# A layer of Mamba, MoE and attention on one core: the Mamba front written out over five turns, its scan's diagonals made by DMA, and the router's normalised rows on ScalarE

## The chip, the cores and the metric

The kernel runs on one core of a Trainium2 chip. A core has TensorE (PE, matrix products and transposes), VectorE (DVE), ScalarE (ACT), GpSimd (POOL) and SyncE (SP), which issues DMA transfers. Each engine works through its own instructions in order, and they wait for each other by semaphores. The metric is the device time of one launch in microseconds (us). Lower is better.

## The reference, cut to what matters

The input x is 8 sequences of 512 tokens with 128 features. Four blocks follow each other, each with its layer norm and residual: Mamba, a mixture of experts, attention, and the same mixture of experts again. The change touches the Mamba block and the first router behind it:

```
x   = x + mamba(layernorm(x))
    xn    = x * rsqrt(mean(x*x) + eps) * norm_w            # x is layernorm(x) here
    x_s,z = split(xn @ in_proj_w.T)                        # 256 channels each
    u     = silu(causal_conv4(x_s) + conv_b)
    dt,B,C = split(u @ x_proj_w.T)                         # 8, 16, 16 columns
    delta = softplus(dt @ dt_proj_w.T + dt_proj_b)
    for each of 16 states s:  h_t = exp(delta*A_s)*h_{t-1} + delta*u*B_s ;  y += h*C_s
    y     = (y + u*D) * silu(z)
    out   = y @ out_proj_w.T + x
x   = x + moe(layernorm(x))     # router: argmax and softmax of layernorm(x) @ gate_w, 8 experts
x   = x + attention(layernorm(x)) ; x = x + moe(layernorm(x))
```

The residual of the Mamba block adds x and layernorm(x), so x is replaced by x(1+rstd) - mean*rstd before the block's output is added.

## The kernel before

Tokens lie on 128 partitions, in 32 tiles (`NT`) of 128 tokens, four of them (`TPB`) to a batch of 512 tokens. Channels number 256, as two chunks (`NC`) of 128 partitions.

**setup** loads x in four parts, takes each tile's mean and variance on DVE (`bn_stats`, then `bn_aggr`, then two copies for each batch), builds the table of the attention bias (`ext`) on DVE, and from the variances the factors `rr` (both reciprocal roots) and `r12`. A barrier ends it.

**mamba_front** computes `u`, the gates `zs`, `delta`, `du` = delta*u and the B columns `bT` of each batch, and leaves all in a large SBUF tile called `arena`. PE, DVE, ACT, POOL and SP each have a loop of hardware (`Fori`) over the batches with peeled first and last turns. In a turn b DVE runs `normed(b+2)` (L424, four tiles), `conved(b+1)` (L451, six operations), `lows(b)` (L479), `deltas` (L463, the positive part of delta), a copy of B (L473), `residual(b+2)` (L438, four tiles of x(1+rstd) - mean*rstd) and `bounds(b)` (L484, the minimum that ends the log1p). POOL does four 128x1024 operations for a batch: L608 and L611 make the log1p's sum from what `lows` left, L614 adds the positive part to give delta, L618 multiplies by u. L614 needs `bounds` of the same batch. `delta_ln`, `delta_low` and `delta_pos` have one buffer each.

**mamba_scan** runs over n = 16b + s: 128 steps, one state s of one batch b each. A step is: ACT scales du by B into `b_du` (L730, four tiles, two buffers) and makes exp(delta*A) in `d_a` (L738, two operations, two buffers); PE transposes the four tiles into PSUM, `p_dbu` (L834, two buffers); DVE scans 128x1024 into `h` (L954, six buffers); POOL multiplies by the C row (L690), which SP has loaded with a DMA for each step (four buffers); PE adds the product up (L854), four steps behind the first. For s in `DIAG` = (1, 3, 11, 15) ACT instead scales four 128x128 identity tiles (a diagonal of B), and PE multiplies du with that diagonal (L831).

Between the steps stands other work on earlier batches, placed by s. For batch b-1: DVE gates the sum at s=2 (L961), copies at s=5, 6, 8 and 9, adds the residual at s=7 (L967), takes the router's moments at s=8; ACT makes the router's `rstd` at s=10; POOL makes the router's normalised rows at s=10 (`pool_rows`, L1246, four tiles); PE turns these rows at s=13 (L1206), ACT copies them at s=14 (L1186), PE forms the logits at s=14 (L1212), ACT copies x at s=15 (L1200). For batch b-2: the rest of the router, ending in four indirect DMAs from POOL at s=7 (`pool_send`, L1259).

The waits that the prediction speaks of are these. `exps` of step n waits for the end of scan n-2 (`scanned, n - 1`), and so does PE's `spread`; scan n waits for `exps` and `spread` of n and for the product n-6 to be added up; each engine takes its own list strictly in order.

## Time and profile before

| | |
|---|---|
| median of 3 runs | 1271.05 us (1267.11 to 1273.8) |
| the profiled execution: its time | 1267.82 us |
| its span, first to last instruction | 1266.0 us |
| around the span | 1.82 us |
| mean granted TensorE clock | 0.948 |
| busy over the span: PE / DVE / ACT / POOL | 84% / 73% / 68% / 42% |
| setup | 0 to about 20 us |
| front | 24.6 us (first work on DVE) to 151.9 us |
| scan | 158.9 us (first scan) to 531.4 us |
| from there: end of the router, experts, attention, experts | to 1266.0 us |

The scan of step 0 of batches 0 to 6 starts at 158.87, 202.60, 247.73, 296.07, 343.01, 390.17 and 437.30 us. Busy shares are averages over stages with unlike limits, so a stage has to be read by itself.

### The profile page before, as it was taken

The page shows a single profiled execution, that of the slowest core. Times are in us where ns is not written, and L with a number is a line of the kernel's source. Part 1 is how long each engine was busy: PE and PEld are TensorE (multiplying, and loading weights), DVE is VectorE, ACT ScalarE, POOL GpSimd, SP SyncE. Part 2 cuts the span into 40 slices and gives each one's busy share as a digit, 9 for nine tenths or more (in the row PEclk, how much of TensorE's full clock was granted, in tenths as well). Part 3 has the DMA queues.
Part 4 walks back from the last instruction along what each step waited for, and adds up shares of the span by engine and source line. Part 5 has one row for each costly group of instructions (what it writes and reads, how often), then busy time and mean ns, then how long its engine had stood idle before and what let it go on. Part 6 is the DMA issues. An engine that isn't in the chain of part 4 may idle for free. (4 is left out here: it accounts for less than half of the span.)

```text
span 1266.0 us, 25040 instructions
## 1 busy us (share of the span) xinstructions
PE 1064.5 (84%) x7486; PEld 758.3 (60%) x7486; DVE 925.9 (73%) x2001; ACT 866.4 (68%) x1837; POOL 533.2 (42%) x361
## 2 busy tenths in 40 slices
PE   1776399988888888769967999998999999993897
PEld 0333278888887888639963455544454545542897
DVE  5899588998898898845644777767685868674565
ACT  1777599999999999635642757565675657661564
POOL 0366478989999999733440001010101010111344
PEclk9988799999999999988997999998999999997899
DMA  3000023233364354223322000000000000001331
GB/s 89 2 2 3 35 77 97 92 96 101 116 204 136 110 187 124 67 75 97 91 72 58 1 2 18 1 19 1 17 0 19 1 17 1 17 18 55 90 89 52
DMA packets 50631, 74.40 MB, mean 59 GB/s; under 512 B 7351, under 2 KB 28604, under 8 KB 50528
## 3 DMA queue, kind: packets, MB, share of 16 engines
q1 hardware_dynamic: 41648, 51.22, 13.9%
q0 software_dynamic: 5568, 12.66, 2.8%
q10 hardware_dynamic: 3312, 9.33, 2.3%
q8 instruction: 41, 0.67, 0.2%
q14 instruction: 62, 0.51, 0.1%
HBM read 57.86 MB, written 16.24 MB: 59 GB/s over the span
## 5 line engine op out<-in xcount | busy, mean ns | idle before, releaser
L954 DVE TENSOR_TENSOR_SCAN h<-d_a,p_dbu 128x1024 f32<-128x1024 f32 x128 | 290.2, 2280 | 37.3 <-ACT d_a L738 33.0
L690 POOL TENSOR_TENSOR h<-h,c_rep 128x1024 f32<-128x1024 f32 x126 | 295.1, 2366 | 25.1 <-DVE h L954 23.7
L1894 ACT ACTIVATE arena<-arena,at_min 128x512 f32<-128x512 f32 x256 | 183.2, 720 | 118.5 <-DVE at_min L2005 114.9
L2005 DVE CUSTOM_DVE_ANT_0 arena<-at_p_scores,arena 128x512 f32<-128x512 f32 x256 | 174.6, 685 | 83.2 <-PE at_p_scores L1769 41.8
L1255 POOL TENSOR_SCALAR r_row<-r_row 128x4 f32<-128x4 f32 x16 | 3.8, 239 | 472.9 <-DVEq L1160 472.9
L1776 PEld LDWEIGHTS at_p_probs_T<-ident,arena 128*128 128x128 f32 x1024 | 113.1, 142 | 97.2 <-issue 73.9
L738 ACT ACTIVATE d_a<-arena,a_exp 128x511 f32<-128x511 f32 x256 | 169.2, 709 | 0.2 <-DVE h L954 0.2
L1769 PE MATMUL at_p_scores<-arena,at_q_T 64*128 64x512 f32 x512 | 161.8, 646 | 6.9 <-DVE at_min L2005 5.3
L1776 PE MATMUL at_p_probs_T<-ident,arena 128*128 128x128 f32 x1024 | 159.0, 284 | 5.2 <-ACT arena L1894 4.8
L730 ACT ACTIVATE b_du_T<-arena,b_T 128x256 f32<-128x256 f32 x384 | 162.6, 495 | 0.1
L854 PE MATMUL p_y_T<-ident,h 128*128 128x128 f32 x1024 | 133.6, 274 | 5.0 <-POOL h L690 4.9
L854 PEld LDWEIGHTS p_y_T<-ident,h 128*128 128x128 f32 x1024 | 115.9, 141 | 7.2 <-POOL h L690 6.6
L834 PE MATMUL p_dbu<-ident,b_du_T 128*128 128x128 f32 x768 | 114.4, 284 | 5.0 <-ACT b_du_T L730 3.5
L2014 DVE COPY at_probs_T<-at_p_probs_T 128x512 f32<-128x512 f32 x128 | 88.1, 688 | 31.2 <-PE at_p_probs_T L1776 31.1
L1861 ACT ACTIVATE at_probs_T<-at_p_probs_T 128x512 f32<-128x512 f32 x128 | 75.6, 591 | 38.4 <-PE at_p_probs_T L1776 36.1
L834 PEld LDWEIGHTS p_dbu<-ident,b_du_T 128*128 128x128 f32 x768 | 86.5, 143 | 22.3 <-ACT b_du_T L730 9.7
L1436 PE MATMUL f_p_h<-f_xg_T,f_w_cur 128*128 128x128 f32 x624 | 88.2, 287 | 5.9 <-DVE f_w_cur L1492 5.5
L1472 ACT ACTIVATE f_h_T<-f_p_h,f_w_cur 128x128 f32<-128x128 f32 x312 | 88.8, 374 | 4.3 <-PE f_p_h L1436 3.4
L1448 PE MATMUL f_p_y<-f_w_cur,f_h_T 128*128 128x128 f32 x624 | 84.2, 279 | 0.7 <-issue 0.7
L1436 PEld LDWEIGHTS f_p_h<-f_xg_T,f_w_cur 128*128 128x128 f32 x624 | 78.9, 199 | 8.5 <-issue 6.8
L1769 PEld LDWEIGHTS at_p_scores<-arena,at_q_T 64*128 64x128 f32 x512 | 43.8, 187 | 61.8 <-issue 45.0
L1448 PEld LDWEIGHTS f_p_y<-f_w_cur,f_h_T 128*128 128x128 f32 x624 | 77.2, 195 | 1.3 <-issue 1.1
(242 smaller groups left out, 1661.3 us busy)
## 6 DMA issues: line engine op xcount, KB each, us to landing
c_rep<-c_rows SPq DMA_DIRECT2D x128, 256.0 KB, 3.2
f_row<-expert_rows SPq DMA_DIRECT2D x78, 129.0 KB
arena<-in_w_all ACTq DMA_DIRECT2D x8, 578.0 KB
arena<-bias_by_distance ACTq DMA_DIRECT2D x8, 448.0 KB
x_tok<-in_x SPq DMA_DIRECT2D x4, 512.0 KB, 5.6
x_tok<-x_between SPq DMA_DIRECT2D x8, 256.0 KB, 2.7
expert_rows<-r_row,r_dest POOLq DMA_INDIRECT x64
expert_rows<-h SPq DMA_DIRECT2D x6, 129.0 KB
```

Source lines behind the costliest of these rows:

```text
L690: nc.gpsimd.tensor_tensor(h[:, n % HS, :, :], h[:, n % HS, :, :], cc, ALU.mult).then_inc(prod_done, 1)
L730: nc.scalar.activation(b_du[:, s % SR, j, 0:width], src, ACT.Copy, scale=bT[:, one(b), j, s:s + 1].squeeze(1)).then_inc(scaled, 1)
L738: nc.scalar.activation(da[:, s % 2, ch, 1:], delta[:, one(b), ch, 1:].squeeze(1), ACT.Exp, scale=a_exp[:, ch, s:s + 1]).then_inc(da_ready, 1)
L834: mm = nc.tensor.transpose(dst, b_du[:, s % SR, j, ch * P:(ch + 1) * P], k.ident[:])
L854: mm = nc.tensor.matmul(p_yT[:, j, ch * P:(ch + 1) * P], h[:, n % HS, ch, j * P:(j + 1) * P], k.ident[:], is_transpose=SUM_BY_TRANSPOSE, s ...
L954: nc.vector.tensor_tensor_scan(h[:, n % HS, :, :].rearrange("p c t -> p (c t)"), da[:, s % 2, :, :].rearrange("p c t -> p (c t)"), p_dbu[: ...
L1436: mm = nc.tensor.matmul(ph[:, r % R, f, :], w_cur[:, r % R, f * P:(f + 1) * P], xgT[:, r % R, :], start=True, stop=True)
L1448: mm = nc.tensor.matmul(py[:, r % YR, 0:D], ht[:, r % R, f, :], w_cur[:, r % R, FF + f * D:FF + (f + 1) * D], start=f == 0, stop=f == FC - 1)
L1769: nc.tensor.matmul(psc[:, n % SCB, :], qT[par][half, hd // 2, it * P:(it + 1) * P], kT[par][half, hd // 2, :], start=True, stop=True).then ...
L1776: mm = nc.tensor.transpose(ppt[:, s % 2, j * P:(j + 1) * P], pr[:, s % RING, j * P:(j + 1) * P], k.ident[:])
L1894: nc.scalar.activation(pr[:, slot, :], sc[:, slot, :], ACT.Exp, scale=-1.0, bias=mn[:, slot:slot + 1]).then_inc(probs_ready, 1)
L2005: V.tensor_tensor_reduce(sc[:, slot, :], psc[:, s % SCB, :], band[:, hd, w0:w0 + T], 1.0, 3.0e38, ALU.add, ALU.min, mn[:, slot:slot + 1]). ...
```

## The change

1. **setup.** `bn_aggr` writes straight into a tile that is kept, its two copies go, and it runs one batch behind `bn_stats`. The bias table is made by ACT (three operations and a negation) and its zeroing by POOL. The factors 1+rstd, -mean*rstd and `rn` are made at the end of setup. The weights of the Mamba block are loaded here, not in the front.
2. **mamba_front.** All loops are written out. Every engine runs through turns i = -3 to 7, in which each piece works on its own batch i + offset. The residual is made before the normalised x: for batches 0 to 3 by DVE in `normed`, for 4 to 7 by ACT, with 16 operations that are the first of the front. `delta_pos` has two buffers, the log1p its own buffer `lm`, and POOL makes delta and du one turn later than the sums.
3. **mamba_scan, diagonals.** For the 30 steps from n=8 on with s in `DIAG` (`BY_DIAG`) ACT makes no diagonal. SP writes four B values of each partition to the diagonals of a 128x128x4 block in DRAM that is zero otherwise (four such blocks, zeroed once at the start), seven steps ahead, and loads the block into `diag_b` four steps ahead (two buffers). Both stand in the queue of the C rows.
4. **mamba_scan, router's rows.** `pool_rows` goes. DVE makes -mean*rstd (128x4) behind scan 10, `stage == 3`, and ACT makes the rows with scale and bias (`act_normed`) behind the exponentials of s=11.

```diff
@@ setup
-                    for j in range(TPB):
-                        ch.step(V.bn_stats(stats[:, b % 2, j, :], k.x[:, g + j, :]))
-                    ch.wait()
-                    for j in range(TPB):
-                        ch.step(V.bn_aggr(mv[:, b % 2, j, :], stats[:, b % 2, j, :]))
-                    ch.wait()
-                    ch.step(V.tensor_copy(k.mean[:, g:g + TPB], mv[:, b % 2, :, 0]))
-                    ch.step(V.tensor_copy(var[:, g:g + TPB], mv[:, b % 2, :, 1]))
+            for b in range(B):
+                if b % (B // PARTS) == 0:
+                    dve.wait_ge(x_in[b // (B // PARTS)], 16)
+                parts_of(b)
+                if b > 0:
+                    moments_of(b - 1, TPB)
@@ mamba_front, the turns
+        def each(*parts):
+            for i in range(-3, B):
+                for ahead, part in parts:
+                    if 0 <= i + ahead < B:
+                        part(i + ahead)
...
+            each((0, dt_proj), (2, project_in), (1, x_proj), (3, turn))                                    # PE
+            each((1, conved), (0, positive), (-1, bounds), (0, take_b), (3, normed), (0, lows))            # DVE
+            each((1, first_tap), (0, xd_out), (2, x_out), (1, gates), (0, absolute), (1, u_out), (0, logs))  # ACT
+            each((0, log_sums), (-1, delta_du))                                                            # POOL
@@ mamba_front, DVE
+            def positive(b):
+                after(dve, delta_done, b - 1)
+                for ch in range(NC):
+                    dve.wait_ge(abs_ready, b * NC + ch + 1)
+                    nc.vector.tensor_scalar(mpos[:, b % 2, ch, :], pdt[:, ch, :], dt_b(ch), 0.0,
+                                            ALU.add, ALU.max).then_inc(pos_ready, 1)
+            def bounds(b):
+                if b == B - 1:
+                    return
+                dve.wait_ge(log_sum_ready, b + 1)
+                after(dve, delta_done, b)
+                nc.vector.tensor_tensor(lm[:], low[:], ex[:], ALU.min).then_inc(log1p_ready, 1)
@@ mamba_front, ACT
+            for g in range(NT // 2, NT):
+                nc.scalar.activation(k.x[:, g, :], k.x[:, g, :], ACT.Identity, scale=k.one_plus[:, g:g + 1],
+                                     bias=k.shift[:, g:g + 1]).then_inc(half_added, 1)
@@ mamba_scan, SP
+            def write_diagonal(i):
+                b, s = divmod(BY_DIAG[i], NS)
+                if i >= DR:
+                    sp.wait_ge(diag_in[(i - DR) % DB], 16 * ((i - DR) // DB + 1))
+                dst = bass.AP(diag_rows.tensor, i % DR * TPB * P * P, [[P + 1, P], [P * P, TPB], [1, 1]])
+                sp.dma_start(dst, bT[:, b, :, s:s + 1], allow_slow_non_contiguous=True).then_inc(diag_out[i % DR], 16)
+            def read_diagonal(i):
+                sp.wait_ge(diag_out[i % DR], 16 * (i // DR + 1))
+                if i >= DB:
+                    sp.wait_ge(dbu_ready, BY_DIAG[i - DB] + 1)
+                sp.dma_start(diag_b[:, i % DB, :, :],
+                             diag_rows[i % DR].rearrange("j k m -> k j m")).then_inc(diag_in[i % DB], 16)
@@ mamba_scan, POOL and ACT
-                    if s == 10 and b > 0:
-                        rt.pool_rows(pool, b - 1)
+                if n in BY_DIAG:
+                    return
...
+                    if number > 0 and s == 11:
+                        rt.act_normed(act, b - 1)
@@ Router
+        elif stage == 3 and self.in_psum:
+            dve.wait_ge(self.rstd_ready, 1 + b)
+            V.scalar_tensor_tensor(out=self.shift, in0=self.mv[:, :, 0], scalar=-1.0, in1=self.rstd,
+                                   op0=ALU.mult, op1=ALU.mult).then_inc(self.shift_ready, 1)
+    def act_normed(self, act, b):
+        act.wait_ge(self.shift_ready, 1 + b)
+        self.rows_out(act, b)
+        for j in range(TPB):
+            ins = self.k.nc.scalar.activation(self.row[:, j, 0:D], self.k.x[:, b * TPB + j, :], ACT.Identity,
+                                              scale=self.rstd[:, j:j + 1], bias=self.shift[:, j:j + 1])
+        ins.then_inc(self.ln_ready, 1)
```

How the order of instructions moves is shown at three places. The first is POOL in the front: before, this is the loop's body (sum of the log1p in L608 and L611, delta in L614, du in L618, all of one batch).

```order
L608 TENSOR_TENSOR delta_low<-delta_e,delta_low 128x1024
L609 REGISTER_ALU
L611 TENSOR_TENSOR delta_low<-delta_low,delta_ln 128x1024
L614 ISA
L614 TENSOR_TENSOR arena<-delta_ln,delta_pos 128x1024
L616 ISA
L618 ISA
L618 TENSOR_TENSOR arena<-arena 128x1024
```

After, POOL's first ten operations of the front are these (L572 and L575 the sums, L563 delta, L566 du).

```order
L572 TENSOR_TENSOR delta_low<-delta_e,delta_low 128x1024
L575 TENSOR_TENSOR delta_low<-delta_low,delta_ln 128x1024
L572 TENSOR_TENSOR delta_low<-delta_e,delta_low 128x1024
L575 TENSOR_TENSOR delta_low<-delta_low,delta_ln 128x1024
L563 TENSOR_TENSOR arena<-delta_log1p,delta_pos 128x1024
L566 TENSOR_TENSOR arena<-arena 128x1024
L572 TENSOR_TENSOR delta_low<-delta_e,delta_low 128x1024
L575 TENSOR_TENSOR delta_low<-delta_low,delta_ln 128x1024
L563 TENSOR_TENSOR arena<-delta_log1p,delta_pos 128x1024
L566 TENSOR_TENSOR arena<-arena 128x1024
```

The sums of a batch now stand directly ahead of delta and du of the batch before it, and DVE's minimum of the earlier batch falls under them. DVE's own turn of the front is this after the change, here a turn that still normalises (L455 `conved`, L468 `positive`, L487 `bounds`, L473 the B columns, L441 `normed`, L479 `lows`).

```order
L455 SCALAR_TENSOR_TENSOR conv<-p_xz,vec,conv 128x511 x2
L455 SCALAR_TENSOR_TENSOR conv<-p_xz,vec,conv 128x510 x2
L455 SCALAR_TENSOR_TENSOR conv<-p_xz,vec,conv 128x509 x2
L468 TENSOR_SCALAR delta_pos<-p_dt,vec 128x512 x2
L487 TENSOR_TENSOR delta_log1p<-delta_low,delta_e 128x1024
L473 COPY b_T<-p_xdbc 128x64
L441 TENSOR_SCALAR xn_tok<-x_tok,mean_and_var,rn 128x128 x4
L479 TENSOR_SCALAR delta_low<-delta_e 128x1024
```

The residual has left the turn, `lows` has gone from its middle to its end, and the minimum stands after `positive`. The second place is ACT in the scan from s=10 to s=15 of a batch: before, with the diagonals from `ident` at s=11 and s=15.

```order
L1182 ACTIVATE r_rstd<-r_lnv 128x4
L738 ACTIVATE d_a<-arena,a_exp 128x511 x2
L730 ACTIVATE b_du_T<-ident,b_T 128x128 x4
L738 ACTIVATE d_a<-arena,a_exp 128x511 x2
L730 ACTIVATE b_du_T<-arena,b_T 128x256 x4
L738 ACTIVATE d_a<-arena,a_exp 128x511 x2
L730 ACTIVATE b_du_T<-arena,b_T 128x256 x4
L738 ACTIVATE d_a<-arena,a_exp 128x511 x2
L730 ACTIVATE b_du_T<-arena,b_T 128x256 x4
L1186 ACTIVATE arena<-p_r_x 128x512
```

After, over the same steps (L722 the scaling, L730 the exponentials, L1192 the router's rows, L1198 the copy at s=14).

```order
L1186 ACTIVATE r_rstd<-r_lnv 128x4
L730 ACTIVATE d_a<-arena,a_exp 128x511 x4
L1192 ACTIVATE r_row<-x_tok,r_veps,r_rstd 128x128 x4
L722 ACTIVATE b_du_T<-arena,b_T 128x256 x4
L730 ACTIVATE d_a<-arena,a_exp 128x511 x2
L722 ACTIVATE b_du_T<-arena,b_T 128x256 x4
L730 ACTIVATE d_a<-arena,a_exp 128x511 x2
L722 ACTIVATE b_du_T<-arena,b_T 128x256 x4
L1198 ACTIVATE arena<-p_r_x 128x512
```

The four diagonal tiles are gone, and four row tiles stand ahead of the scaling of s=12. The third place is DVE behind scan 10, after the change (L953 is the scan; before, the same list has no L1115 and the scans stand in one row).

```order
L974 COPY arena<-p_r_x 128x2x256
L953 SCALAR_TENSOR_TENSOR h<-d_a,p_dbu 128x1024
L974 COPY arena<-p_r_x 128x2x256
L953 SCALAR_TENSOR_TENSOR h<-d_a,p_dbu 128x1024
L1115 SCALAR_TENSOR_TENSOR r_veps<-r_mv,r_rstd 128x4
L953 SCALAR_TENSOR_TENSOR h<-d_a,p_dbu 128x1024 x4
```

One small operation with both inputs in SBUF now stands between scan 10 and scan 11.

## Rows read from the trace of the kernel before

**Rows 1.** Windows: busy us by engine, one batch of the scan (s=10 to s=10).
```profile
373.29:420.45 47.16, 41.45 (x356) 38.41 (x355) 42.24 (x45) 45.29 (x102) 44.71 (x26) 1.00 0.44 139
```

**Rows 2.** Timeline, DVE, setup and first turn: start, us, engine, line, operation, count [idle before].
```profile
5.08 0.87 DVE L246 BATCH_NORM_STATS2 n_stats<-x_tok 128x6 f32<-128x128 f32 x4 [1.73 <-DMA x_tok<-in_x]
...
19.38 0.19 DVE L268 TENSOR_TENSOR r<-rstd_and_rms 128x32 f32<-128x32 f32 x1 [0.61 <-ACT rstd_and_rms L223]
...
24.84 1.11 DVE L424 TENSOR_SCALAR xn_tok<-x_tok,mean,r 128x128 f32<-128x128 f32 x4
...
47.76 0.69 DVE L479 TENSOR_SCALAR delta_low<-delta_e 128x1024 f32<-128x1024 f32 x1 [0.62 <-ACT delta_e L577]
```

**Rows 3.** Timeline, PE, first projections of the front.
```profile
28.01 3.78 PE L368 MATMUL p_xz<-xn_T,w_in 128*128 128x512 f32 x4 [0.83 <-ACT xn_T L536]
...
31.59 3.20 PE L362 MATMUL p_xz<-w_in,xn_T 128*128 128x256 f32 x8
```

**Rows 4.** Timeline, DVE, one turn of the front's loop.
```profile
76.32 0.68 DVE L479 TENSOR_SCALAR delta_low<-delta_e 128x1024 f32<-128x1024 f32 x1
76.92 1.40 DVE L463 TENSOR_SCALAR delta_pos<-p_dt,vec 128x512 f32<-128x512 f32 x2
...
78.37 4.09 DVE L438 TENSOR_SCALAR x_tok<-x_tok,one_plus_rstd,mean_rstd  x4
82.37 1.22 DVE L484 TENSOR_TENSOR delta_ln<-delta_low,delta_e 128x1024 f32<-128x1024 f32 x1
...
86.58 4.02 DVE L451 SCALAR_TENSOR_TENSOR conv<-p_xz,vec,conv 128x511 f32<-128x511 f32 x6
```

**Rows 5.** Timeline, POOL, the same turn.
```profile
77.08 2.36 POOL L608 TENSOR_TENSOR delta_low<-delta_e,delta_low 128x1024 f32<-128x1024 f32 x1 [2.39 <-DVE delta_low L479]
...
86.70 2.37 POOL L618 TENSOR_TENSOR arena<-arena  x1 [0.38 <-POOL arena L614]
```

**Rows 6.** One line: ns min/median/max of one, first and last start (us).
```profile
L1012 DVE TENSOR_TENSOR h<-h,c_rep x2: 1212/1468/1723, 531.5 to 533.2; 128x1024 f32<-128x1024 f32 x2
```

**Rows 7.** Timeline, POOL, the end of the scan.
```profile
522.90 9.29 POOL L690 TENSOR_TENSOR h<-h,c_rep 128x1024 f32<-128x1024 f32 x4
```

**Rows 8.** Timeline, DVE, the last operation of the front.
```profile
150.68 1.23 DVE L520 TENSOR_TENSOR arena<-arena 128x1024 f32<-128x1024 f32 x1
```

**Rows 9.** Timeline, DVE, scans 10 to 13, 14, 15 and 0.
```profile
373.29 8.88 DVE L954 TENSOR_TENSOR_SCAN h<-d_a,p_dbu 128x1024 f32<-128x1024 f32 x4
384.20 2.29 DVE L954 TENSOR_TENSOR_SCAN h<-d_a,p_dbu 128x1024 f32<-128x1024 f32 x1 [2.03 <-ACT d_a L738]
...
387.79 2.29 DVE L954 TENSOR_TENSOR_SCAN h<-d_a,p_dbu 128x1024 f32<-128x1024 f32 x1 [1.22 <-ACT d_a L738]
...
390.17 2.28 DVE L954 TENSOR_TENSOR_SCAN h<-d_a,p_dbu 128x1024 f32<-128x1024 f32 x1
```

**Rows 10.** Timeline, ACT, s=14 to s=1 of the same batch.
```profile
382.35 0.60 ACT L1186 ACTIVATE arena<-p_r_x 128x512 f32<-128x512 f32 x1 [0.91 <-PE p_r_x L1206]
...
385.76 1.32 ACT L738 ACTIVATE d_a<-arena,a_exp 128x511 f32<-128x511 f32 x2
386.98 1.69 ACT L730 ACTIVATE b_du_T<-arena,b_T 128x256 f32<-128x256 f32 x4
388.58 1.33 ACT L738 ACTIVATE d_a<-arena,a_exp 128x511 f32<-128x511 f32 x2
389.81 1.27 ACT L730 ACTIVATE b_du_T<-ident,b_T 128x128 f32<-128x128 f32 x4
```

**Rows 11.** Timeline, POOL, s=10 on, and behind the next batch's indirect DMAs.
```profile
378.40 3.14 POOL L1246 TENSOR_SCALAR r_row<-x_tok,r_mv,r_rstd 128x128 f32<-128x128 f32 x4
381.52 27.98 POOL L690 TENSOR_TENSOR h<-h,c_rep 128x1024 f32<-128x1024 f32 x12
...
418.52 4.71 POOL L690 TENSOR_TENSOR h<-h,c_rep 128x1024 f32<-128x1024 f32 x2
```

**Rows 12.** DMA issues: KB each, median us from issue to landing.
```profile
c_rep<-c_rows SPq DMA_DIRECT2D x128, 256.0 KB, 3.2
```

More of the change, by code:

```diff
@@ L263, in _, with parts_of, moments_of @@
-            ch.link(V.tensor_scalar(args[:, 0, :], var[:], LN_EPS, None, ALU.add))
+            def parts_of(b):
+                for j in range(TPB):
+                    ch.step(V.bn_stats(stats[:, b, j, :], k.x[:, b * TPB + j, :]))
+            def moments_of(b, back):
+                ch.wait(back)
+                for j in range(TPB):
+                    ch.step(V.bn_aggr(k.mv[:, b * TPB + j, :], stats[:, b, j, :]))
+            for b in range(B):
[4 more added lines that the diff above has]
+                    moments_of(b - 1, TPB)
@@ L332, in _ @@
[L332 to L340 removed]
+            for b in range(B):
+                sp.wait_ge(xd_ready, b + 1)
+                sp.dma_start(cscr[b], xd[C_AT:C_AT + NS, :]).then_inc(c_stored, 16)
@@ new lines, in project_z, with project_in @@
+            def project_z(b):
+                pe.wait_ge(xnT_ready, b + 1)
+                after(pe, z_taken, b * NC)
+                for j in range(TPB):
+                    at = j % 2 * DI
+                    mm = nc.tensor.matmul(pz[:, NC + j // 2, at:at + DI], xnT[:, j * P:(j + 1) * P], w_in[:, DI:],
+                                          start=True, stop=True)
+                    if j % 2:
+                        mm.then_inc(z_half_ready, 1)
+            def project_in(b):
+                if b == 0:
+                    project_x(b)
+                    project_z(b)
+                else:
+                    project_z(b)
+                    project_x(b)
@@ L419, in normed @@
             def normed(b):
-                dve.wait_ge(xT_ready, b)
+                if b < B // 2:
+                    for g in range(b * TPB, b * TPB + TPB):
+                        chn.step(nc.vector.tensor_scalar(k.x[:, g, :], k.x[:, g, :], k.one_plus[:, g:g + 1],
+                                                         k.shift[:, g:g + 1], ALU.mult, ALU.add))
+                    chn.wait()
+                else:
+                    dve.wait_ge(half_added, (b - B // 2 + 1) * TPB)
+                after(dve, xT_ready, b)
@@ L431, in residual @@
-            def residual(b):
-                dve.wait_ge(xn_ready, b + 1)
-                chn.wait()
-                for j in range(TPB):
-                    g = b * TPB + j
-                    xg = k.x[:, one(g), :].squeeze(1)
-                    chn.step(nc.vector.tensor_scalar(xg, xg, rone[:, one(g)], mr[:, one(g)],
-                                                     ALU.mult, ALU.subtract))
+                ins.then_inc(xn_ready, 1)
             def conved(b):
@@ L487, in _ @@
-            residual(0)
-            conved(0)
-            normed(1)
-            residual(1)
-            def turn(b, conv_next=True, norm_next=True):
-                if norm_next:
-                    normed(b + 2)
-                if conv_next:
-                    conved(b + 1)
-                lows(b)
-                deltas_and_b(b)
-                if norm_next:
-                    residual(b + 2)
-                bounds(b)
-            with dve.Fori(0, B - 2) as b:
-                chn.begin(b, 11)
-                turn(b)
@@ L629, in mamba_scan @@
     DIAG = (1, 3, 11, 15)
+    BY_DIAG = [n for n in range(NS // 2, B * NS) if n % NS in DIAG]
+    DR, DB = 4, 2
     HALF = T // 2
```

346 lines of the change are left out of this document (146 added, 200 removed).

## Prediction

> **What bounds the kernel now.** I read the page's slices first: no engine is busy throughout, so the stages were read apart, by windows and then by timelines of one turn and one batch. About 0.5% (6.4 us) is what a measurement of this kernel can tell from no change.
>
> In the front DVE sets the pace. A turn takes 14.21 us (`lows` at 76.32 [rows 4], the next `lows` at 90.53, which is 86.58 + 3.95 [rows 4]). The reader is to see that much of it is not DVE's own work: four x_tok operations take 4.09 us [rows 4], where four like them take 1.11 us with POOL idle [rows 2]. POOL is at its 128x1024 operations then [rows 5], so a DVE operation from SBUF to SBUF waits for the end of POOL's operation. Operations that read PSUM show nothing of it: the six of conv take 4.02 us, 0.67 each, with POOL at L618 from 86.70 on [rows 4, 5].
>
> In the scan a batch takes 47.16 us (373.29 to 420.45), with ACT busy 45.29, POOL 44.71, DVE 42.24, PE 41.45 of it [rows 1]. Scans 10 to 13 follow each other at 2.22 us; then DVE stalls 2.03 and 1.22 us ahead of scans 14 and 15 [rows 9]. The chain behind that: POOL makes the router's rows at 378.40 to 381.52 [rows 11], PE turns them, ACT waits 0.91 us for it [rows 10], and the exponentials of s=14 stand behind that copy.
>
> **The change, part by part.**
>
> *Setup.* Now a batch of statistics takes 0.87 us for four [rows 2] within a period of 1.46; without copies and waits I take 1.13. With the bias table gone from DVE (0.9) and 0.8 added at the end for the new factors, DVE ends at about 17.2 instead of 19.57 [rows 2]. A barrier costs 1.1 us (150.68 + 1.23 = 151.91 [rows 8], next block 153.0). The weights are there, so the front begins at 18.3, not at 24.8 [rows 2]: 6.5 us earlier.
>
> *Start of the front.* The 6.5 us don't arrive. ACT's 16 residual tiles come first: a 128x128 tile costs 0.29 (four in 1.27 with their overlap [rows 10]), so 4.7 us, until 23.0. The first projection starts at about 23.7 instead of 28.01 [rows 3], 4.3 earlier. But x_proj(0) now stands behind the whole projection of batch 1, whose two halves take 3.78 and 3.20 us at the low clock of the start [rows 3], about 5 us as the clock rises, and `gates(0)` ahead of `u_out(0)`. Following the lists I put x_dbc(0) at 40.1 and `lows(0)`'s end at 48.1. Before it ended at 48.45 [rows 2]. Gain 0.3.
>
> *A turn.* Turn 1 is ACT's: its list adds up to 10.8 us with two table loads; `lows(1)` ends at 59.0. From turn 2 on POOL and DVE form a loop. Count from the end of `lows(i-1)`: two sums, delta(i-2) and du(i-2), each 2.36 and 0.08 apart, 0.38 ahead of du [rows 5]: delta done at 7.3, du running from 7.7 to 10.1. `positive(i)` waits for delta(i-2) (two buffers) and takes until 8.7 (1.40 for two, less 0.07 of overlap [rows 4]). Next is `bounds`, with both inputs in SBUF. Does POOL hold it up? Its 1.22 in the loop [rows 4] doesn't tell, since POOL then waits for it. L1012 does: of two equal products one takes 1212 ns and the other, begun at 531.5, 1723 ns [rows 6], and POOL's last product ended at 522.90 + 9.29 = 532.19 [rows 7]. 532.19 plus 1.2 is 533.4, near its end at 533.25. So `bounds` runs from 10.1 to 11.3; the copy of B, four unblocked `normed` (1.11 [rows 2]) and `lows` (0.68 [rows 4]) end at 13.25. ACT's exponential waits for `bounds` and is done at 12.5, in time. Turns 2 to 4 take 13.25, turns 5 and 6 (no `normed`, but that exponential) 13.15. In turn 7 delta(6) holds `lows(7)` until 13.7, du(6) holds the first operation of the tail until 16.7, and five operations of 1.23 [rows 8] end 22.85 after `lows(6)`. Sum: 59.0 + 39.75 + 26.3 + 22.85 = 147.9 against 151.9 [rows 8]. The front gives 4.0 us. Were `bounds` not held, a turn would take 11.9 and the tail less: 138, a gain of 14.
>
> The Trainium skill states the lock in so many words (SBUF — State Buffer, "SBUF: two separate sides"): VectorE with two SBUF inputs, or in a two-port mode, and GpSimd each take a shared pair of ports for a whole instruction, and the other waits. It speaks against this change; by it the front gives the smaller figure. The trace agrees, 1723 against 1212 ns.
>
> *Diagonals.* ACT loses 4 x 0.29 = 1.17 us in 30 steps. In batch 0, where ACT alone sets the pace (2.82 a step: 1.22 from 385.76 to 386.98 and 1.60 on to 388.58 [rows 10]), both steps count: 43.7 becomes 41.4, -2.3. SP's new transfers are each issued steps ahead. Their cost is not in the trace; the nearest row is a C row's 3.2 us for 256 KB [rows 12], the same size as a diagonal's load. Zeroing hides under the wait for the first product. At s=15 the C row stands behind a load that waits for `spread(15)`, which makes POOL's product some 1.8 us late where PE needs it 3 steps later: nothing. Low bound 0; high bound, were a write of 512 single elements to take three times 3.2 us, about 1 us a batch from SP's blocked C rows, 7 us. I take 0.
>
> *Router's rows.* POOL loses 3.1 us [rows 11] and the stall of 2.03 + 1.22 goes. In its place comes a wait: the small operation stands behind scan 10, and ACT, which would have scaled s=12 under scan 10, waits for it. Count from scan 10's end. The small operation has two SBUF inputs, and POOL is catching up behind its indirect DMAs, back to back from 418.52 at 2.33 a product [rows 11] (27.98 for twelve [rows 11]); its second ends at 423.2, scan 10 (420.45, the end of [rows 1]) at 422.7: held 0.5. Rows 0.7 to 1.9; scaling 12 to 3.5; exponentials 12 ready at 4.8, where scan 12 could have begun at 2.8: stall 2.0. ACT then needs 2.82 a step for 13 and 14 against 2.22 of the scan, and the copy of s=14 between: scans 13, 14, 15 and 0 begin at 7.7, 11.0, 13.3 and 15.7. Before, scan 0 began 14.7 after scan 10's end (390.17 - 375.5 [rows 9]). So +1.0. From s=0 to s=10 DVE's own list and its wait for the gate, which hangs on PE and on `scanned`, take what they took; two stalls of 0.2 and 0.24 for late diagonals may go: -0.3 to -0.4. A batch: +0.6 or +0.7. Batch 1, ACT-bound at 45.1 (starts listed with the profile), comes to 45.7: +0.6. Batch 2, 48.3 before, to 47.8: -0.5. Batches 3 to 7: +3.5. With batch 0's -2.3 the scan comes to +1.3.
>
> *Behind the scan* nothing is changed; POOL's products end earlier, but DVE's chain after scan 15 is its own.
>
> Sum: -4.0 + 1.3 = -2.7. Against the profiled execution's 1267.8 that is 1265.1; the median of the runs lies 3.2 above that execution, so 1268.
>
> **The rivals.**
>
> 1. *`bounds` isn't held* (0.2). Against it: [rows 6, 7], though one operation is thin. -14 in the front instead of -4: 1258.
> 2. *The scan falls to POOL's pace* (0.1). POOL's load after the change is 16 x 2.33 + 6.0 for the send = 43.3 a batch, ACT's 41.8, DVE's 42.3. If the wait for scan 10 hid, six batches would give 3.7 each, -22: 1245. For it: all four engines would be below 43.5. Against: the count above, each step of it in program order.
> 3. *Slower: the small operation is held for a whole product* (0.15). If POOL has just begun a product at scan 10's end, DVE and ACT wait 2.3 instead of 0.5, 1.8 more in each of 7 batches: +12.6, 1281. Place: L1115. It decides from a hold of 1.8 us on average on (0.5 + (6.4 + 2.7)/7). For it: POOL's phase was worked out to 0.3 us only.
> 4. *The diagonals come late* (0.05): SP stands at a write's receipt, POOL waits for C rows: +7, 1275.
>
> The forecast, both locks as counted, has 0.5.
>
> **How the numbers follow.** Within the forecast's case the start of the front is uncertain by 3 us and a batch by 0.5 (3.5 in all), so its own range is 1262 to 1274, of which 0.2 lies below 1264.7, the bound of faster. The range for 8 in 10 reaches to rival 1 below, with 4 us of its own, and takes half of rival 3 above: 1254 to 1279. Faster: 0.1 + 0.2 (rival 1) + 0.1 (rival 2) - a little = 0.38. Slower (above 1277.4): rival 3, a part of rival 4 and 0.02 of the forecast: 0.17. Same: 0.45.
>
> **What would show it.** In the profile after: DVE's first `normed` at 18 to 19 us; the first 128x1024 operation of POOL at 48; L487 taking about 2.5 us from its start, its end just behind L566's end, and POOL's L572 13.2 us apart; a first scan at 155. In the scan: no b_du_T from ident after n=3, a stall of 2.0 at scan 12 put down to ACT's d_a, small ones at 13 and 14, L1115 longer than 0.2 us, ACT idle ahead of L1192 by 1.5 us, and batches of 47.5 to 48. Wrong it would be if L487 takes 1.2 us with POOL busy beside it, if scan 12 begins 2.3 us behind scan 11, or if POOL waits for c_rep.

## The result, and the profile after

| | before | after |
|---|---|---|
| median | 1269.68 us (1267.11 to 1273.8, 4 runs) | 1290.38 us (1288.4 to 1294.2, 4 runs) |
| the profiled execution: its time, its span | 1267.82, 1266.0 us | 1289.68, 1287.9 us |
| mean granted TensorE clock | 0.948 | 0.923 |
| first scan begins | 158.87 us | 148.88 us |
| first scan to the end of the last | 372.6 us | 406.7 us |
| from there to the end | 734.5 us | 732.3 us |

The change makes the kernel slower: the ratio of the times is 1.0164, 95% interval 1.0126 to 1.0201. That is clear of the noise, and about 2% at the most. The table splits the difference of the spans, +21.9 us: -10.0 before the first scan, +34.1 in the scan, -2.2 behind it. Forecast were -4.0, +1.3 and 0.

The scan gains in batch 0 alone. It loses 1.2 us in batch 1 and 4.6 to 6.5 us in each batch from there on. These are windows of the kernel after (columns as in [rows 1]), from one step-0 scan to the next to within 0.06 us, for batches 0 to 3. Before, the same four took 43.73, 45.13, 48.34 and 46.94 us.

```profile
148.88:191.23 42.35, 38.44 (x272) 32.98 (x272) 37.09 (x19) 41.93 (x88) 34.89 (x15) 0.85 0.42 113
191.23:237.47 46.24, 41.53 (x350) 38.19 (x349) 41.17 (x35) 42.38 (x88) 37.95 (x17) 1.00 0.42 115
237.47:290.44 52.97, 42.13 (x356) 40.37 (x354) 47.70 (x46) 42.49 (x89) 41.93 (x22) 0.94 0.38 110
290.44:343.87 53.43, 42.89 (x356) 41.34 (x354) 47.40 (x46) 42.60 (x89) 41.80 (x22) 0.90 0.40 109
```

In batch 3 DVE is busy 47.40 us where it was 42.24 [rows 1], though it got one small operation more. A busy time that grows by far more than the work added points to an instruction that is held while it counts as executing. The timeline of DVE around scan 10 of a batch shows which; it answers to [rows 9].

```profile
320.29 2.28 DVE L953 TENSOR_TENSOR_SCAN h<-d_a,p_dbu 128x1024 f32<-128x1024 f32 x1
322.48 5.18 DVE L1115 SCALAR_TENSOR_TENSOR r_veps<-r_mv,r_rstd 128x4 f32<-128x4 f32 x1
327.58 2.27 DVE L953 TENSOR_TENSOR_SCAN h<-d_a,p_dbu 128x1024 f32<-128x1024 f32 x1
332.20 2.29 DVE L953 TENSOR_TENSOR_SCAN h<-d_a,p_dbu 128x1024 f32<-128x1024 f32 x1 [2.34 <-ACT d_a L730]
335.33 2.29 DVE L953 TENSOR_TENSOR_SCAN h<-d_a,p_dbu 128x1024 f32<-128x1024 f32 x1 [0.84 <-PE p_dbu L833]
```

The same stretch on POOL and on ACT (these answer to [rows 11] and [rows 10]):

```profile
318.35 9.28 POOL L683 TENSOR_TENSOR h<-h,c_rep 128x1024 f32<-128x1024 f32 x4
330.00 2.36 POOL L683 TENSOR_TENSOR h<-h,c_rep 128x1024 f32<-128x1024 f32 x1 [2.37 <-DVE h L953]
...
319.83 1.34 ACT L730 ACTIVATE d_a<-arena,a_exp 128x511 f32<-128x511 f32 x2 [1.01 <-DVE h L953]
327.69 1.65 ACT L1192 ACTIVATE r_row<-x_tok,r_veps,r_rstd 128x128 f32<-128x128 f32 x4 [6.53 <-DVE r_veps L1115]
```

The reader is to see four things. An operation on four elements a partition takes 5.18 us. It ends at 327.66, which is the end of POOL's run of four products (318.35 + 9.28 = 327.63), and not the end of the product under way at its start (the second, which ends near 323.0). ACT stands for 6.53 us, since its rows need L1115, and everything of s=12 stands behind them. And when DVE goes on, the stall at scan 12 that the prediction expected comes on top (2.34).

POOL's run ends there because nothing is left for it: its next product (330.00) has sat idle 2.37 us for scan 11, and scan 11 stands behind L1115. So the hold is as long as the backlog that POOL has when L1115 begins, here the rest of one product and two more. What put POOL behind is the router's send, 312.38 to 318.34 in this batch.

Over all batches the line's row (ns min/median/max) says how often:

```profile
L1115 DVE SCALAR_TENSOR_TENSOR r_veps<-r_mv,r_rstd x7: 136/5154/6127, 221.9 to 533.5; 128x4 f32<-128x4 f32 x7
```

The 0.14 us is batch 1, where nothing of the router's send has yet put POOL behind; there the batch took 46.3. In the other six it ends within 0.04 us of the end of a run of four products. The seven take 32.3 us together, 31.3 more than seven of 0.14.

The hold has an echo on PE. Windows of the kernel after around it:

```profile
318.00:322.00 4.00, 4.00 (x38) 3.97 (x37) 4.00 (x3) 2.15 (x4) 3.99 (x3) 1.00 0.14 48
322.00:327.60 5.60, 0.77 (x8) 0.53 (x5) 5.60 (x3) 0.00 (x0) 5.60 (x3) 0.83 0.71 165
327.60:333.00 5.40, 3.12 (x15) 3.08 (x16) 3.06 (x3) 5.31 (x13) 2.39 (x2) 0.50 0.20 64
```

PE works 0.77 of 5.60 us, and in the next stretch the granted clock is 0.50, its lower level (1.2 GHz). Eight transposes of s=12 then take 1.94 us, where those of s=9 took 1.04. This is why scan 13 waits 0.84 us for PE above, where it waited 0.54 for ACT in batch 1. The echo is small and doesn't come each time: after holds of the same length scan 13 waits 0.84 or 0.85 us in batches 3, 5 and 7, and 0.54 in batches 2, 4 and 6.

**The front** did better than forecast. DVE's turn after the change, and POOL's of the same turn, answer to [rows 4] and [rows 5]:

```profile
81.61 0.69 DVE L479 TENSOR_SCALAR delta_low<-delta_e 128x1024 f32<-128x1024 f32 x1
83.37 4.04 DVE L455 SCALAR_TENSOR_TENSOR conv<-p_xz,vec,conv 128x511 f32<-128x511 f32 x6 [1.06 <-ACT conv L519]
89.53 1.41 DVE L468 TENSOR_SCALAR delta_pos<-p_dt,vec 128x512 f32<-128x512 f32 x2 [2.12 <-POOL arena L563]
90.86 2.15 DVE L487 TENSOR_TENSOR delta_log1p<-delta_low,delta_e 128x1024 f32<-128x1024 f32 x1
92.93 0.21 DVE L473 COPY b_T<-p_xdbc 128x64 f32<-128x64 f32 x1
93.06 1.10 DVE L441 TENSOR_SCALAR xn_tok<-x_tok,mean_and_var,rn 128x128 f32<-128x128 f32 x4
94.19 0.69 DVE L479 TENSOR_SCALAR delta_low<-delta_e 128x1024 f32<-128x1024 f32 x1
```

```profile
82.38 2.36 POOL L572 TENSOR_TENSOR delta_low<-delta_e,delta_low 128x1024 f32<-128x1024 f32 x1 [3.04 <-DVE delta_low L479]
84.82 2.37 POOL L575 TENSOR_TENSOR delta_low<-delta_low,delta_ln 128x1024 f32<-128x1024 f32 x1
87.13 2.37 POOL L563 TENSOR_TENSOR arena<-delta_log1p,delta_pos 128x1024 f32<-128x1024 f32 x1
89.58 2.35 POOL L566 TENSOR_TENSOR arena<-arena 128x1024 f32<-128x1024 f32 x1
```

A turn takes 12.58 us (94.19 - 81.61), against 14.21 before. `bounds` (L487) takes 2.15 us and ends at 93.01, 1.08 behind the end of POOL's du (89.58 + 2.35 = 91.93): it is held, as forecast. In turn 1, with POOL idle, it took 1.21.

### The profile page after: what moved, and what is told of

It is laid out like the page before. It is cut to its first block and busy times, and to the rows that moved or that the text cites. A ratio compares the mean times of both kernels' runs of the same rounds, so it can differ in the third digit from the quotient of the medians.

```text
span 1287.9 us, 24549 instructions
## 1 busy us (share of the span) xinstructions
PE 1060.4 (82%) x7470; PEld 769.1 (60%) x7470; DVE 929.8 (72%) x1974; ACT 851.3 (66%) x1764; POOL 513.8 (40%) x335
## 5 line engine op out<-in xcount | busy, mean ns | idle before, releaser
L953 DVE TENSOR_TENSOR_SCAN h<-d_a,p_dbu 128x1024 f32<-128x1024 f32 x128 | 291.0, 2280 | 40.4 <-ACT d_a L730 33.1
L730 ACT ACTIVATE d_a<-arena,a_exp 128x511 f32<-128x511 f32 x256 | 169.2, 710 | 16.6 <-DVE h L953 16.6
L722 ACT ACTIVATE b_du_T<-arena,b_T 128x256 f32<-128x256 f32 x392 | 165.9, 495 | 0.1
L833 PE MATMUL p_dbu<-ident,b_du_T 128*128 128x128 f32 x784 | 119.9, 298 | 51.5 <-DVE h L953 45.3
L853 PE MATMUL p_y_T<-ident,h 128*128 128x128 f32 x1024 | 138.9, 281 | 1.2 <-DVE h L1011 1.1
L833 PEld LDWEIGHTS p_dbu<-ident,b_du_T 128*128 128x128 f32 x784 | 97.5, 152 | 62.3 <-DVE h L953 48.8
L853 PEld LDWEIGHTS p_y_T<-ident,h 128*128 128x128 f32 x1024 | 122.1, 146 | 1.7 <-DVE h L1011 1.7
```

What stands on the lines that cost most here:

```text
L722: nc.scalar.activation(b_du[:, s % SR, j, :], du_T(b, j), ACT.Copy, scale=bT[:, one(b), j, s:s + 1].squeeze(1)).then_inc(scaled, 1)
L730: nc.scalar.activation(da[:, s % 2, ch, 1:], delta[:, one(b), ch, 1:].squeeze(1), ACT.Exp, scale=a_exp[:, ch, s:s + 1]).then_inc(da_ready, 1)
L833: mm = nc.tensor.transpose(dst, b_du[:, s % SR, j, ch * P:(ch + 1) * P], k.ident[:])
L853: mm = nc.tensor.matmul(p_yT[:, j, ch * P:(ch + 1) * P], h[:, n % HS, ch, j * P:(j + 1) * P], k.ident[:], is_transpose=SUM_BY_TRANSPOSE, s ...
L953: nc.vector.tensor_tensor_scan(h[:, n % HS, :, :].rearrange("p c t -> p (c t)"), da[:, s % 2, :, :].rearrange("p c t -> p (c t)"), p_dbu[: ...
```

## The experiments

Theory A, formed from these rows: nearly the whole loss is the hold of L1115, which lasts until POOL stops issuing product after product. Its two forms are that the lock passes at the first gap between two of POOL's operations, however short (A1), and that it passes only when POOL has no work ready (A2). The rivals: ScalarE's rows themselves, with the wait behind scan 10, cost the time; or the diagonals by DMA do. Ratios are to the kernel before on the same chip, whose median was 1268.69 us in the first four runs (7 runs) and 1267.47 us in the last three (22 runs).

**e1_psum_mean.** If the hold needs both inputs in SBUF, it must go when one of them is moved. The negated mean is copied to PSUM at s=8, and L1115's successor (L1122) reads it there. With the sign gone into the copy it is a TENSOR_TENSOR and no longer a SCALAR_TENSOR_TENSOR.

```diff
+            if self.in_psum:
+                dve.wait_ge(self.var_ready, 1 + b)
+                ts(self.minus_mean, self.mv[:, :, 0], -1.0, None, ALU.mult).then_inc(self.mean_moved, 1)
...
-            V.scalar_tensor_tensor(out=self.shift, in0=self.mv[:, :, 0], scalar=-1.0, in1=self.rstd,
-                                   op0=ALU.mult, op1=ALU.mult).then_inc(self.shift_ready, 1)
+            dve.wait_ge(self.mean_moved, 1 + b)
+            tt(self.shift, self.minus_mean, self.rstd, ALU.mult).then_inc(self.shift_ready, 1)
```

> The changed kernel with one edit: the router's mean is first moved to PSUM (negated, 128x4, behind the moments at s=8), and the small product behind scan 10 reads it there, so that it has one input in SBUF instead of two. Theory A (the lock: with two SBUF inputs that operation is held until POOL's run of products ends, 5.2 us in six batches): it takes about 0.15 us, scan 11 follows scan 10 at 2.3 to 2.4, a batch falls from 53.2 to 47.3 to 47.8, the time from 1290 to 1254 to 1258. Rival B (the place: DVE and ACT meet behind scan 10, and the hold only fills a wait that is there anyway): the operation gets short, but the batch stays above 50 and the time above 1272. Rival C (the diagonals' transfers make the batch long): as B.

Measured: 1259.95 us (1258.32 to 1261.27), ratio 0.9932, interval 0.9913 to 0.9951. The operation's row in this kernel:

```profile
L1122 DVE TENSOR_TENSOR r_veps<-p_r_small,r_rstd x7: 135/136/136, 221.9 to 508.9; 128x4 f32<-128x4 f32 x7
```

One input moved out of SBUF gives 30 us back (1290.4 to 1260.0, 2 us above the range expected) and turns a slower kernel into a faster one. The batches from step-0 scan to step-0 scan now take 42.3, 46.5, 47.8, 48.2, 47.8, 48.2 and 47.9. POOL is in the same kind of run (products from 313.56 to 322.89) when L1122 executes at 317.95, and it takes 0.14 us in the middle of it. The new kind of instruction isn't what frees it, since L487 of the front is a TENSOR_TENSOR with two SBUF inputs and was held (2.15 against 1.21). What follows is theory A, and both rivals together can hold no more than what is left.

**e4_gap.** The changed kernel with a gap between POOL's products: each waits for the end of the one before. The operation L1117 is L1115 as it was, both inputs in SBUF.

```diff
+                    if n > 0:
+                        pool.wait_ge(prod_done, n)
```

> The changed kernel with one wait more: POOL waits for the end of its previous product before each product, so that its products no longer follow each other without a gap (some 0.05 to 0.1 us between them); the small product keeps its two SBUF inputs. Theory A1 (the lock is passed on at the first gap between two of POOL's operations): the small product is held for the rest of one product, 0.1 to 2.4 us instead of 5.2; a batch takes 48 to 50.5 and the time is 1262 to 1275. Theory A2 (it is passed on only when POOL has nothing more to run): 5 us as now, 1290 or a little more.

Measured: 1263.75 us (1262.97 to 1264.71), ratio 0.9958, interval 0.9942 to 0.9975, at the lower end of A1's range. POOL and DVE of this kernel, and the line's row:

```profile
316.32 2.40 POOL L685 TENSOR_TENSOR h<-h,c_rep 128x1024 f32<-128x1024 f32 x1
318.89 2.35 POOL L685 TENSOR_TENSOR h<-h,c_rep 128x1024 f32<-128x1024 f32 x1 [0.17 <-POOL h L685]
321.41 2.35 POOL L685 TENSOR_TENSOR h<-h,c_rep 128x1024 f32<-128x1024 f32 x1 [0.17 <-POOL h L685]
...
319.81 1.44 DVE L1117 SCALAR_TENSOR_TENSOR r_veps<-r_mv,r_rstd 128x4 f32<-128x4 f32 x1
321.18 2.27 DVE L955 TENSOR_TENSOR_SCAN h<-d_a,p_dbu 128x1024 f32<-128x1024 f32 x1
...
L1117 DVE SCALAR_TENSOR_TENSOR r_veps<-r_mv,r_rstd x7: 135/1029/1614, 222.6 to 514.1; 128x4 f32<-128x4 f32 x7
```

POOL's products now stand 0.17 us apart. The small operation begins inside the product that ends at 321.24, and ends at 321.25: a gap of 0.17 us is enough for it, with POOL's next product ready. The median hold falls from 5.0 to 0.9 us, and 27 of the 30 us come back though POOL has become slower. In each of the five batches in which L1117 was held it ended within 0.02 us of the end of the one product under way. A2 falls, and A1 is what these products show. This is also the state that the prediction had assumed for the kernel as it is.

**e2_pool_rows.** The changed kernel with the router's rows on POOL again and no L1115; front and DMA-made diagonals as in the change.

```diff
+                    if s == 10 and b > 0:
+                        rt.pool_rows(pool, b - 1)
...
-                    if number > 0 and s == 11:
-                        rt.act_normed(act, b - 1)
...
-            EARLY = {0: 8, 1: 8, 3: 10, 4: 14, 5: 15}
+            EARLY = {0: 8, 1: 8, 4: 14, 5: 15}
```

> The changed kernel with the router's rows back on POOL at s=10 (no small product behind scan 10, none of the four ACT tiles at s=11); new front and diagonals by DMA stay. Theory A: the loss is all in the moved rows; a batch is what POOL needs, 46.5 to 47.2, the front keeps its 10 us: 1255 to 1260. Rival C (the diagonals' transfers cost): batches stay above 49, time above 1272.

Measured: 1255.64 us (1253.39 to 1258.57), ratio 0.9890, interval 0.9873 to 0.9908. The batches: 42.3, 43.2, 47.0, 46.7, 46.7, 46.7, 46.7. It lies in the range of theory A, rival C falls, and it is the fastest of all kernels here.

**e3_front_only.** e2 with all diagonals by ACT from `ident`, as before: of the change only the setup and the front are left.

```diff
-    BY_DIAG = [n for n in range(NS // 2, B * NS) if n % NS in DIAG]
+    BY_DIAG = []
...
-                    nc.scalar.activation(b_du[:, s % SR, j, :], du_T(b, j), ACT.Copy,
+                    src, width = (k.ident[:], P) if s in DIAG else (du_T(b, j), DI)
+                    nc.scalar.activation(b_du[:, s % SR, j, 0:width], src, ACT.Copy,
```

> The changed kernel with the rows back on POOL and all diagonals by ACT as before: of the change only setup and front are left. All theories: the first scan starts 10 us earlier (149 instead of 159), the batches are those of before (47.1), time 1259 to 1261. If the front's gain is lost again behind it (a colder TensorE clock at the scan's start, 0.50 in the stretch 128 to 160 us after the change), the first batch is longer and the time 1263 or more. Against the run with rows on POOL and diagonals by DMA it gives the diagonals' own worth: I expect 1 to 3 us in their favour.

Measured: 1261.61 us (1261.2 to 1263.17), ratio 0.9945, interval 0.9928 to 0.9963. The batches: 43.7, 45.1, then 48.6, 46.7, 47.2, 47.1, 47.1, those of the kernel before. So setup and front are worth 7 us of the median, and the diagonals by DMA another 6 to 7 (0.9945 to 0.9890), where I had expected 1 to 3. By the first scan's start the front gives 10.3 (148.5 against 158.87); where the rest goes isn't settled. Behind the scan this execution took 739.0 us against 734.5 before, with the same instructions, and the others of this study 731 to 738, so a part of the span alone can't be read closer than some 5 us there.

**e5_before_lone.** Does the hold need the change at all? The kernel before, with the one operation behind scan 10, into a tile that nothing reads.

```diff
-            EARLY = {0: 8, 1: 8, 4: 14, 5: 15}
+            EARLY = {0: 8, 1: 8, 3: 10, 4: 14, 5: 15}
...
+        elif stage == 3 and self.in_psum:
+            dve.wait_ge(self.rstd_ready, 1 + b)
+            V.scalar_tensor_tensor(out=self.lone[:], in0=self.mv[:, :, 0], scalar=-1.0, in1=self.rstd,
+                                   op0=ALU.mult, op1=ALU.mult).then_inc(self.lone_done, 1)
```

> The kernel before, with one operation more in each batch from the second on: behind scan 10 DVE forms -mean*rstd (128x4, both inputs in SBUF) into a tile of its own that nothing reads. It waits for the rstd of ScalarE as in the changed kernel. Nothing else is altered: the rows stay on GpSimd, the diagonals on ScalarE, the front in its loops. Theory (the small operation waits until GpSimd's back-to-back run of products ends): GpSimd is in such a run at scan 10 in the later batches, so the operation takes 2 us or more in most of batches 2 to 7, often about 5, and scan 11 starts later by as much. The loss is at most 6 x 5 = 30 us, and probably less, since the exponentials of s=11 and s=12 are made meanwhile and the stalls of 2.03 and 1.22 at s=14 and s=15 can take up part: I expect 10 to 25 us more than before, 1280 to 1294. Rival (the loss of the changed kernel needs ScalarE's rows or the front's order, and a two-input operation of this size alone costs its own 0.14 us): under 3 us, 1268 to 1272.

Measured: 1276.56 us (1274.9 to 1280.66, 9 runs), ratio 1.0066, interval 1.0044 to 1.0089: 8.4 us more (5.6 to 11.3 by the interval). The median misses the range of 10 to 25 from below, and is clear of the rival's 3. DVE and POOL of this kernel at one place, and the line's row:

```profile
332.27 2.96 DVE L1117 SCALAR_TENSOR_TENSOR r_lone<-r_mv,r_rstd 128x4 f32<-128x4 f32 x1
...
328.17 7.03 POOL L690 TENSOR_TENSOR h<-h,c_rep 128x1024 f32<-128x1024 f32 x3
335.17 3.14 POOL L1252 TENSOR_SCALAR r_row<-x_tok,r_mv,r_rstd 128x128 f32<-128x128 f32 x4
...
L1117 DVE SCALAR_TENSOR_TENSOR r_lone<-r_mv,r_rstd x7: 273/2954/4125, 235.8 to 527.4; 128x4 f32<-128x4 f32 x7
```

The operation ends at 335.23 and POOL's run of three products at 335.20, where POOL's own rows begin (L1252). So it was again held past a product's end (332.89) to the end of the products. But it got its turn although the trace shows no gap there: L1252 begins at 335.17. Its wait (for `rstd`, long met) is no explanation, since each product too has waits ahead of it that are met. It is the same in all six batches with a hold. So a gap is enough for the turn to pass (e4), but it isn't the only thing that passes it, and what does it here stays open. The hold is shorter than after the change; and nothing on ACT hangs on this operation, so of 18.5 us held (19.4 in all, less seven of 0.14) only 8.4 reach the end. In the changed kernel, whose ACT waits for it, 30 of 31.3 do.

**e6_psum_act_diag.** e1 with all diagonals by ACT: the edit to the diagonals is that of e3.

> e1_psum_mean (the changed kernel with the negated mean in PSUM) with all diagonals made by ScalarE from the identity again, none by DMA. The result is the same. With the rows on GpSimd the DMA-made diagonals were worth 1261.6 - 1255.6 = 6.0 us. With the rows on ScalarE, that engine has 3 us more of work in each of seven batches, and the diagonals 1.17 us a batch more. If ScalarE sets the pace then, the diagonals are worth more than 6: 1.17 x 8 = 9.4 at the most, 1269. If the engine has room where the diagonals lie (s=11 and s=15 beside the rows, s=1 and s=3 not), about 6 again: 1266. If the diagonals by DMA cost anything in transfers there, less: 1263.

Measured: 1271.57 us (1269.02 to 1274.0, 12 runs), ratio 1.0029, interval 1.0011 to 1.0046. With the rows on ACT the diagonals by DMA are worth 0.0097 of the time (1.0029 - 0.9932), 12 us, twice as much as with the rows on POOL and more than the 9.4 that I had put as the most. That bound was miscounted: 1.17 us is what one diagonal costs ACT, and there are 30 of them, four in a batch. By the profiles ACT is busy 883.5 us here and 850.5 in e1, 33 us more, so 12 breaks no bound. The 3 us for the rows were wrong too: that is POOL's time for them, and ACT makes the four in 1.65 us. A batch takes 49.4 to 49.8 us against 47.1 in e3 and 47.9 in e1. ACT is the engine that both edits load or relieve, and their costs don't add: the rows on ACT cost 2.4 us a batch with its own diagonals, 1.2 without (47.9 against 46.7 in e2).

**e7_psum_early.** e1 with `rstd` made at s=9 and the shift behind scan 9, so that ACT's rows needn't wait for scan 10.

```diff
-                if s == 10 and after_scale:
+                if s == 9 and after_scale:
...
-            EARLY = {0: 8, 1: 8, 3: 10, 4: 14, 5: 15}
+            EARLY = {0: 8, 1: 8, 3: 9, 4: 14, 5: 15}
```

> e1_psum_mean with rstd made by ScalarE at s=9 and the shift -mean*rstd by DVE at s=9, both one step earlier; the rows stay on ScalarE behind the exponentials of s=11. The result is the same. The predicted chain said that ScalarE's rows wait for scan 10's end, that the scaling and the exponentials of s=12 stand behind them, and that scan 12 stalls by 2.0 us for that (2.35 in e1_psum_mean). With the shift ready one scan earlier the rows follow the exponentials of s=11 at once, and these end about when scan 10 begins or shortly after. If that chain is right, the stall at scan 12 falls to under 0.8 and a batch gains 1 to 1.5 us, since ScalarE's own list (2.82 a step with full scaling) then sets scans 13 and 14: time 1250 to 1254, ratio to before about 0.987. If ScalarE's total work sets the batch whatever the order, the stall moves to scans 13 to 15 and nothing is gained: 1259 to 1261. If the wait of the DVE for rstd now shows (made at s=9, asked for behind scan 9), a little is lost: 1262.

Measured: 1260.05 us (1257.96 to 1263.95, 8 runs), ratio 0.9931, interval 0.9907 to 0.9954: no different from e1 (0.9932). DVE's scans 9 to 13 in this kernel, and ACT ahead of `rstd`:

```profile
317.53 2.29 DVE L953 TENSOR_TENSOR_SCAN h<-d_a,p_dbu 128x1024 f32<-128x1024 f32 x1 [1.03 <-ACT d_a L730]
...
320.38 4.46 DVE L953 TENSOR_TENSOR_SCAN h<-d_a,p_dbu 128x1024 f32<-128x1024 f32 x2
325.94 2.29 DVE L953 TENSOR_TENSOR_SCAN h<-d_a,p_dbu 128x1024 f32<-128x1024 f32 x1 [1.10 <-ACT d_a L730]
328.76 2.29 DVE L953 TENSOR_TENSOR_SCAN h<-d_a,p_dbu 128x1024 f32<-128x1024 f32 x1 [0.53 <-ACT d_a L730]
...
315.74 0.30 ACT L1190 ACTIVATE r_lnv<-r_mv,r_eps 128x4 f32<-128x4 f32 x1 [4.13 <-DVE r_mv L1106]
```

The stall of 2.35 at scan 12 has split into 1.10 there and 1.03 at scan 9, since `rstd`, now one step earlier, stands ahead of the exponentials of s=9 and waits for the moments. The first expectation fails. The time is that of the second, but the stall went to scan 9 and not to scans 13 to 15, and ACT isn't at work throughout: it stands 4.13 us at one place, where in e1 it stood 1.30, 1.23 and 1.50 us at three. So this edit has put one wait in the place of another. It doesn't show what the batch would take if neither wait were there.

The ratios lay the change out part by part: setup and front -0.0055, diagonals by DMA -0.0055, rows on ACT with the operation not held +0.0042, the hold +0.0232 (1.0164 - 0.9932; each is a ratio to the kernel before on its own chip). Times 1269 us that is -7, -7, +5 and +29, +21 in all. The shares hang on the order in which the parts are taken out: with the rows on ACT the diagonals are worth 12, not 7.

## Why the prediction was wrong

**The step that failed** is in *Router's rows*: "back to back from 418.52 at 2.33 a product; its second ends at 423.2, scan 10 at 422.7: held 0.5". It took for granted that DVE gets its turn at the end of the product under way. POOL's phase was right: that product ended 0.5 to 0.9 us after L1115 had begun in batches 2 to 6. The turn didn't pass there. Measured was 5.0 to 5.3 us, until the end of a run of four, in five of seven batches (5.18 less 0.14 in the one shown), and 6.0 in the last. The mechanism was there, and its size was ten times what I gave it. The spans differ by 21.9 us where -2.7 was forecast, 24.6 apart. Of these the hold makes +27.4: the scan takes 406.7 us with it and 375.8 without (e1), 30.9 more, where I had 7 times 0.5. The rest of the scan makes +5.4, the front -6.0, and what is behind the scan -2.2.

**Why the rows did not say it.** I had the price from L1012 [rows 6], begun at 531.5 against POOL's end at 532.19 [rows 7]. That row is one of a run of four products, and L1012 began in the fourth: the end of the product and the end of the run are the same moment there. The evidence fits both readings, and I wrote down one. The front's rows [rows 4, 5] show POOL's operations with a gap between, so no run. There the turn does pass at a product's end: the first x_tok operation of the kernel before ends at 79.52, 0.08 behind L608 (77.08 + 2.36 = 79.44), and POOL's next operation begins 0.08 behind it too.

```profile
78.37 1.15 DVE L438 TENSOR_SCALAR x_tok<-x_tok,one_plus_rstd,mean_rstd  x1
...
79.52 2.34 POOL L611 TENSOR_TENSOR delta_low<-delta_low,delta_ln 128x1024 f32<-128x1024 f32 x1
```

The scan's POOL was back to back in [rows 11], which stood in front of me as a fact about load and not about the lock.

The Trainium skill (SBUF — State Buffer, "SBUF: two separate sides") says that whichever starts first has the pair of ports for the whole instruction. By that sentence the hold would be at most one product, 2.33 us less what had passed; the runs show 5.0 and 6.0 where POOL ran its products back to back, and under 1.5 with a gap of 0.17. The measurement decides.

**Rival 3** put the hold at a whole product, 2.3 us, for +12.6 and 0.15. It named the right place and the wrong ceiling. Its point of decision (1.8 us on average) was passed by 2.7 (31.3 / 7 = 4.5). Rival 2 did not happen: in e1 the scan is at 47.9 a batch, not 43.5. Of rival 4 the sign came and not the price. "If POOL waits for c_rep" was to show the forecast wrong, and POOL does wait for a C row at the start of each batch from 1 on, seven times and 15.4 us in all; this is one:

```profile
292.66 16.59 POOL L683 TENSOR_TENSOR h<-h,c_rep 128x1024 f32<-128x1024 f32 x7 [2.19 <-DMA c_rep<-c_rows]
```

Neither the kernel before nor e6, without the diagonals' transfers, has such a wait. It is the 1.8 us that the forecast itself had counted at s=15 (1.7 to 2.8 measured), so as a sign against the forecast it was ill chosen. The lateness is made good within the batch: ahead of each send POOL stands idle for DVE again (0.80 us at 310.05), so that it doesn't add to the backlog at scan 10. A write of 512 single elements landed in 3.5 us and a diagonal's load in 4.0 (medians), near the C row's 3.2 and not three times that.

**The rest of that chain was nearly right.** In batch 1, which had no hold, scans 12, 13, 14, 15 and 0 began 4.7, 7.5, 10.8, 13.2 and 15.6 us after the start of L1115 (221.89), at the end of scan 10; forecast were 4.8, 7.7, 11.0, 13.3 and 15.7, with 0.5 of hold in each. So without a hold the chain is 0.4 longer than I made it. The rows are what it lacked: I gave the four of them 1.2 us, after [rows 10], and ACT took 1.65 (L1192). In e1 the later batches take 47.8 to 48.2 us, where the forecast less its 0.5 is 47.3. With batch 0's 0.9 and batch 1's 1.3 this is the 5.4 above.

**The front**: -10.0 against -4.0, the second mis-sized term. `lows(0)` ended at 46.69 (forecast 48.1), `lows(1)` at 57.14 (10.45 later, forecast 10.9), five turns of 12.57 followed (forecast 13.25 or 13.15), and the tail took 22.0 (forecast 22.85). The most of the turn's 0.6 to 0.7 is one gap: du begins 0.08 us behind delta (89.58), where I had kept the 0.38 of [rows 5]. In both kernels du needs the delta of its own batch. But before, POOL's program had the register instructions of its loop between the two (L616 and L618, 86.36 to 86.60), and written out it has none. Delta ends 0.1 earlier besides, and `bounds` ends 1.08 and not 1.2 behind du. Rival 1 (no hold) is refuted: 2.15 us against 1.21 unheld.

**The diagonals**: no loss by the transfers shows, as taken. Batch 0 came to 42.3 and not 41.4: for n=1 and n=3 ACT now scales full tiles (four of 0.50 us each time, where four from the identity take 0.39), which I had missed. That comes to about 0.8 of the 0.9. Scan 5 waits 2.0 us for PE, but so did scan 1 before, 1.9. In e2 batches 1 and 2 gained 2.0 and 1.6 (against e3), where I had given them next to nothing: ACT's load counts there too. By the medians the diagonals are worth 6 to 7 us (e2 against e3), where the forecast gave them 4.4 (2.3 in batch 0, some 0.35 in each of six more).

**What was not settled:** why the front's 10 us at the first scan are 7 in e3's median; why of the 33 us that the diagonals by DMA take off ACT 12 reach the end with the rows on ACT and 6 to 7 with them on POOL; and what passes the turn in e5, where no gap is to be seen.

## What to carry to other kernels

Before putting an operation with two SBUF inputs on DVE, however small, look at what POOL does at that moment: if its operations follow each other without a gap, count the hold to the end of the whole run, which is as long as POOL's backlog, and ask what hangs on the result. Either take one input from PSUM (30 us here for one copy of 128x4 a batch), or make POOL wait for the end of its own last operation (27 us here for one line), or leave the work where it was (the fastest kernel here keeps the router's rows on POOL, 1255.6 us). And when one row is to carry a price, ask which second reading it would fit as well: an event at the last operation of a run can't tell the operation from the run.
